# A decoder layer on one core: expert sums, sorted rows' transposes, mask waits and the last chunk's loads in another order

## What is computed

```python
    x = _layernorm(x + _L0_attn_ref(x, ...), axis=-1)                 # mixer: conv, GRU, feed-forward
    x = _layernorm(x + _L0_xattn_ref(x, ctx_1024, ctx_1024, ...), axis=-1)
    x = _layernorm(x + _L0_ffn_ref(x, ...), axis=-1)                  # shared expert + top 2 of 16
    # in the cross-attention
        scores = jnp.einsum('bthd,bshd->bhts', q, k)
        scores = scores + NEG_INF * (1.0 - causal)
        attn = jax.nn.softmax(scores, axis=-1)
        out = jnp.einsum('bhts,bshd->bthd', attn, v).reshape(B, T, H * Dv) @ Wo + bo
    # in the experts
        router_logits = jax.nn.sigmoid(x @ gate_w + gate_b)
        expert_values, expert_indices = jax.lax.top_k(router_logits, k=TOP_K)
        return x + _mlp(x, shared_wg, shared_wu, shared_wd) + expert_weighted
```

## Time and profile before

| | |
|---|---|
| time, median of 3 runs | 1507.69 us (1501.65 to 1508.32) |
| the profiled execution | 1508.78 us, its span 1507.0 us |
| PE busy | 1313.7 us (87%) |
| PE weight loads | 1079.7 us (72%) |
| DVE, ACT, POOL busy | 990.8 (66%), 939.4 (62%), 840.4 (56%) us |
| mean granted TensorE clock | 0.965 of full speed |
| PE's longest waits in total | 35.3 us for ACT's exponentials, 24.9 for POOL's xn, 21.1 for DVE's L1416 |

### The profile page before, as it was taken

The page is one execution under the profiler, slowest core; times in us unless marked ns, Lnnn a source line. Parts: engine busy times, 40 slices in busy tenths (PEclk is TensorE's granted clock), DMA queues, the critical chain, the costliest instruction groups (busy, mean ns, idle before and its releaser), DMA issues. The chain is left out here.

```text
span 1507.0 us, 34476 instructions
## 1 busy us (share of the span) xinstructions
PE 1313.7 (87%) x11280; PEld 1079.7 (72%) x11280; DVE 990.8 (66%) x2616; ACT 939.4 (62%) x3395; POOL 840.4 (56%) x988
## 2 busy tenths in 40 slices
PE   2889897989999999989999898989989899998752
PEld 1667686778787787767787787767778787777642
DVE  3456656565666767767776767677676777767535
ACT  2676766576675767577675667667666757756321
POOL 5343445653456555665476655676466645757454
PEclk9999999999999999999999999999999999999877
DMA  7000000033022222133121321223221331225673
GB/s 222 8 8 8 8 8 15 18 86 88 22 75 73 70 72 64 50 92 92 36 77 54 102 79 40 65 87 89 60 65 54 96 98 36 68 81 163 190 213 87
DMA packets 149426, 109.99 MB, mean 73 GB/s; under 512 B 12737, under 2 KB 144385, under 8 KB 149249
## 3 DMA queue, kind: packets, MB, share of 16 engines
q1 hardware_dynamic: 139328, 89.43, 20.4%
q0 software_dynamic: 8192, 16.79, 4.1%
q10 hardware_dynamic: 1728, 1.57, 0.4%
HBM read 73.14 MB, written 34.60 MB: 71 GB/s over the span
## 5 line engine op out<-in xcount | busy, mean ns | idle before, releaser
L1798 POOL TENSOR_TENSOR pr<-pr,ri 128x480 f32<-128x480 f32 x256 | 253.6, 1008 | 305.0 <-DVE ri L1399 303.1
L1073 ACT ACTIVATE pr<-sE,nm 128x120 f32<-128x120 f32 x512 | 178.0, 359 | 248.6 <-DVE nm L1394 247.7
L1073 ACT ACTIVATE pr<-sO,nm 128x120 f32<-128x120 f32 x512 | 179.3, 383 | 0.0
L672 PEld LDWEIGHTS sE<-kT,qT 64*128 64x128 f32 x1024 | 126.4, 191 | 53.8 <-issue 53.8
L705 PE MATMUL pvb<-pT,vv 120*64 120x128 f32 x2048 | 144.1, 284 | 22.2 <-DVE xa L1416 21.1
L1409 DVE TENSOR_TENSOR hT<-pvb,col 128x512 f32<-128x512 f32 x128 | 88.0, 687 | 109.0 <-PE pvb L705 108.4
L1061 ACT ACTIVATE pT<-t 120x512 f32<-120x512 f32 x256 | 143.3, 628 | 24.4 <-PE t L531 24.4
L672 PE MATMUL sO<-kT,qT 64*128 64x120 f32 x1024 | 150.4, 288 | 0.0
L672 PE MATMUL sE<-kT,qT 64*128 64x120 f32 x1024 | 150.4, 288 | 0.0
L705 PEld LDWEIGHTS pvb<-pT,vv 120*64 120x64 f32 x2048 | 116.6, 141 | 47.1 <-issue 42.7
L1827 POOL DMA_INDIRECT sorted_x<-x,slot x128 | 130.3, 1018 | 33.6 <-issue 33.2
(11 more groups left out here) (382 smaller groups left out, 3541.4 us busy)
## 6 DMA issues: line engine op xcount, KB each, us to landing
wq<-in_w_e SPq DMA_DIRECT2D x232, 128.0 KB
sorted_y<-yq SPq DMA_DIRECT2D x68, 256.0 KB, 2.6
xq<-sorted_x SPq DMA_DIRECT2D x58, 256.0 KB, 3.0
xt<-in_x SPq DMA_DIRECT2D x16, 256.0 KB, 3.0
sorted_x<-yq SPq DMA_DIRECT2D x16, 256.0 KB, 4.1
cT<-in_ctxT SPq DMA_DIRECT2D x16, 240.0 KB, 3.1
out_y<-y SPq DMA_DIRECT2D x48, 64.0 KB, 1.6
sorted_x<-x,slot POOLq DMA_INDIRECT x128
```

The lines of the kernel that those rows point to most:

```text
L672: ins = mm(score_banks[r][:, i * S:(i + 1) * S], qT[r * DK:(r + 1) * DK, j, q * T:(q + 1) * T], kT[r * DK:(r + 1) * DK, j, q * S:(q + 1) * ...
L1073: ins = f(pr[:, p % RING, r, i, :], score_banks[r][:, i * S:(i + 1) * S], ACT.Exp, bias=nm[:, p % 2, r, i:i + 1], accum_out=rsum[:, p % 2, ...
L1798: GP.tensor_tensor(pr[:, p % RING, r, :, :], pr[:, p % RING, r, :, :], ri[:, p % 2, r, :, :].to_broadcast([P, 4, S]), ALU.mult).then_inc(s ...
```

## The change

Six edits. (1) `b_scores`: each mask waits for its own bank's exponentials, not for both. (2) In slot 3 of bodies that have stages a and d, `d_T` of the next quad stands ahead of `b_scores`, no longer behind `b_pv`. (3) DVE: with one group in stage e, `e_sum` of the odd slots 3, 5, 7, 9 stands ahead of `b_heads_T` and the reciprocals, no longer behind `d_act`. (4) The two reciprocals of 128x4 are one of 128x8, which waits for both banks' exponentials; both `b_normal` wait for it. (5) SP in the tail: the six `x_load` of the last chunk stand ahead of `d_store(LAST + 3)` and the third `w_load`. (6) The last group's stores of sequences 1 and 3 are issued by ACT, those of 0 and 2 by SP.

```diff
@@ SP, tail
             w_load(n + 1)
+            for i in range(LONE_QUADS):
+                x_load(n + i)
             d_store(LAST + 3)
             w_load(n + 2)
-            for i in range(LONE_QUADS):
-                x_load(n + i)
...
-            for e in (TAIL + 2, TAIL + 3):
-                for q in range(SEQ):
-                    e_store(e, q)
+            for q in range(SEQ):
+                e_store(TAIL + 2, q)
+            for q in range(0, SEQ, 2):
+                e_store(TAIL + 3, q)
@@ PE, b_scores
-                if p:
-
-                    pe.wait_ge(sem["probs"], upto("probs", b, 2 * p - 1))
                 for r in range(2):
+                    if p:
+                        pe.wait_ge(sem["probs"], upto("probs", b, 2 * p - 2 + r))
                     mm(score_banks[r][:, 0:4 * S], identb[:], maskb[:].unsqueeze(1).to_broadcast([P, 4, S]),
@@ PE, body
                         b_probs_T(b, s - LAG)
+                    if up_in(d, s + 1) is not None and s == 3 and A:
+                        d_T(up_in(d, s + 1))
                     if B and 0 < s < PAIRS:
                         b_scores(b, s)
...
-                    if up_in(d, s + 1) is not None:
+                    if up_in(d, s + 1) is not None and not (s == 3 and A):
                         d_T(up_in(d, s + 1), c if s == 1 else None)
@@ ACT, end
+            for q in range(1, SEQ, 2):
+                act.wait_ge(sem["ln3_out"], upto("ln3_out", G - 1, q))
+                act.dma_start(out[(G - 1) * SEQ + q], y_of(G - 1, q)).then_inc(sem[f"out{q}_stored"], 16)
@@ DVE
-            def b_recips(b, p, r):
-                dve.wait_ge(sem["probs"], upto("probs", b, 2 * p + r))
-                V.reciprocal(ri[:, p % 2, r, :, :], rsum[:, p % 2, r, :, :]).then_inc(sem["rinv"], 1)
+            def b_recips(b, p):
+                dve.wait_ge(sem["probs"], upto("probs", b, 2 * p + 1))
+                V.reciprocal(ri[:, p % 2, :, :, :], rsum[:, p % 2, :, :, :]).then_inc(sem["rinv"], 1)
...
+                    if len(es) == 1:
+                        for e, q in sums_in(es, s):
+                            e_sum(e, q)
                     if B and s >= LAG:
                         b_heads_T(b, s - LAG)
                     if B and s < PAIRS:
-                        b_recips(b, s, 0)
-                    if B and s < PAIRS:
-                        b_recips(b, s, 1)
+                        b_recips(b, s)
...
-                    for e, q in sums_in(es, s):
-                        e_sum(e, q)
+                    if len(es) == 2:
+                        for e, q in sums_in(es, s):
+                            e_sum(e, q)
@@ POOL
             def b_normal(b, p, r):
-                pool.wait_ge(sem["rinv"], upto("rinv", b, 2 * p + r))
+                pool.wait_ge(sem["rinv"], upto("rinv", b, p))
```

More of the change, by code:

```diff
@@ L103 @@
     "ctx_hi": 1, "ctx_split": 1, "proj": 24, "proj_act": 12, "proj_dve": 12, "scores": 16, "negmax": 16, "probs": 16,
-    "probsT": 16, "probsT0_sb": 8, "probsT1_sb": 8, "rinv": 16, "normal": 16, "pv": 8, "headsT_sb": 8,
+    "probsT": 16, "probsT0_sb": 8, "probsT1_sb": 8, "rinv": 8, "normal": 16, "pv": 8, "headsT_sb": 8,
     "wo": 4, "attn_sum": 4, "ln2_stats": 4, "ln2_mv": 4, "ln2_eps": 4, "ln2_rstd": 4, "ln2_out": 4,
```

## The result

The changed kernel takes 1514.45 us (median of 7 runs, 1512.92 to 1516.96); the kernel before took 1507.69 us beside it. The ratio is 1.0051, 95% interval 1.0032 to 1.007: slower by half a percent, where 1497 us was forecast. The profiled execution lasted 1514.69 us.

The account below looks back on a forecast made before the run. PE's work plus its waits bound the kernel; +4.5 - 4.1 - 10 + 7.7 - 4.1 - 1.8 - 3.2 - 0.5 = -11.5 us against 1508.8 us gave 1497.3, predicted as 1497 us; own range 1492 to 1502, with rivals 1487 to 1511 us.

Parts of the forecast that it names:

- Slot 3, +4.5 us: Slot 3: bank masks and early transposes gain 0.6 us, but PE then waits for xn: +0.3 us in each of 15 bodies.
- The clock, -4.1 us: Slot 3, even bodies: clock falls cost 8.2 us; cutting PE's standstill in pieces takes half back, bounds 0 and -8.2 us.
- rival (a): Clock falls as before or at other places, so the 4.1 us stay: 1501.5 us, chance 0.17.
- Slots 5 and 6, -10 us: Slots 5 and 6: expert sum moves into DVE's idle time, so PE's waits for L1416 shrink by 10 us.
- a bound of -4 us: Slots 5 and 6: the smallest gain allowed there, if ACT's tanh is the next limit.
- Slots 7 and 8, +7.7 and -4.1 us: Earlier sum delays hT, PE waits 0.77 us in ten bodies; five waits of 0.82 us for xn in slot 8 go.
- The sorting chain, 0 us: Slot 1, even bodies: cast L1511 behind POOL's products, no change taken; bounds -0.8 and +1.0 us in seven bodies.
- rival (c): POOL's two products, released together, hold DVE at L1511 in slot 1 and the sum in slot 7: 1519 us, chance 0.14.
- L1511 over 1.1 us: Slot 1: the sign by which DVE would be seen waiting for both of POOL's products.
- Other masks, -1.8 us: Nine mask waits outside those of slot 3 in bodies 3 to 14 gain 0.2 us each.
- Tail, -3.2 and -0.5 us: Tail: rows loaded earlier let `d_up` start 3.2 us sooner; last four stores issued by two engines gain 0.5 us.
- rival (d): Tail: the loads only swap places, because the DMA engines are full: 1500 us, chance 0.08.

Follow-up runs that it names:

- a1_after: The changed kernel itself, run again on a chip as fast as the first: 1511.35 us, 1.0057 of the kernel before.
- c2: The kernel before with only the tail's two edits (rows' loads ahead of the third weights load, last stores on two engines), on a slower chip: 0.9997 of before.

## Why the prediction was wrong, point by point

Each term against the traces on the faster chip, before and after:

- **Slot 3, +4.5 us.** Right in kind, and in its working: the wait for xn was put at 0.9 us and reads 0.97 us. The slot costs 0.3 us in odd bodies (0.13 + 0.97 against 0.78) and 0.14 us in even ones, +2.6 us in bodies 5 to 14 and about nothing in bodies 0 to 4.
- **The clock, -4.1 us.** Wrong, and rival (a) right: 55 us at the half level ahead of the last scores, before and after. In this trace slot 3 of bodies 4 to 14 no longer falls, but slot 6 does, behind waits of 1.06 and 0.61 us. Windows of slots 3 and 6 in two even bodies (length, PE busy, granted clock, DMA share, GB/s):

```profile
751.00:761.00 10.00, 7.22 (x74) 1.00 0.17 48
925.00:935.00 10.00, 7.21 (x74) 1.00 0.17 49
...
777.00:787.00 10.00, 8.68 (x78) 0.83 0.10 28
951.00:961.00 10.00, 8.68 (x78) 0.83 0.10 28
```

  All four even bodies from 8 to 14 read so in this trace. In the second one of the same kernel (a1_after) slot 3 falls in bodies 4 and 14 in spite of mask and transposes, and slot 6 in bodies 8 and 10 only. Its body 14, slot 3, and bodies 8 and 12, slot 6:

```profile
1274.00:1284.00 10.00, 8.77 (x75) 0.83 0.19 48
777.00:787.00 10.00, 8.32 (x77) 0.83 0.14 42
1125.00:1135.00 10.00, 8.34 (x97) 1.00 0.17 50
```

  With two reciprocals PE waits 1.03 and 0.61 us at the same place in slot 6 and its clock stays. So neither the length of one wait nor what fills it decides alone; what does is not settled. The Trainium skill (TensorE: Matmul & The Clock Gate, Part 4: PE-mode transpose) says that transposes don't count as busy. Slot 3 with the transposes in its wait stayed at 1.00 in one trace and fell in two of six even bodies of the other, and the E mask, a matmul, was there too, so no run here shows it.
- **Slots 5 and 6, -10 us.** This step failed most: the waits for L1416 fell by 5.7 us in bodies 5 to 14 (1.07 us in each odd body, hardly anything in most even ones), and rose by 1.1 us in bodies 0 to 4. The text had a bound of -4 us, where ACT's tanh is next, and I took body 3 as the nearest row instead. In even bodies the next limit is POOL. In slot 5 of body 8, DVE's first operation on the tanh and POOL's operation beside it, before:

```profile
775.71 0.84 DVE L1320 TENSOR_SCALAR hin<-hin 128x512 f32<-128x512 f32 x1
775.07 1.20 POOL L1754 TENSOR_TENSOR cS_lo<-cT,cS_hi 128x480 fp32r<-128x480 f32 x1
```

  and in the changed kernel, with DVE up to L1421:

```profile
773.25 1.40 DVE L1325 TENSOR_SCALAR hin<-hin 128x512 f32<-128x512 f32 x1 [1.26 <-ACT hin L1015]
774.69 0.69 DVE L1327 SCALAR_TENSOR_TENSOR hin<-ma,hin 128x512 f32<-128x512 f32 x1
...
776.14 0.66 DVE L1399 TENSOR_REDUCE nm<-sE 128x4 f32<-128x480 f32 x1
776.71 0.65 DVE L1399 TENSOR_REDUCE nm<-sO 128x4 f32<-128x480 f32 x1
777.28 0.28 DVE L1421 TENSOR_TENSOR xa<-pvb,x1b 128x128 f32<-128x128 f32 x1
...
773.17 1.20 POOL L1761 TENSOR_TENSOR cS_lo<-cT,cS_hi 128x480 fp32r<-128x480 f32 x1
```

  DVE is now idle for 1.26 us for the tanh, a time which the sum used to fill. Behind the reciprocal L1325 does start 0.56 us earlier than before (1.46 us after it, not 2.02), but it takes 1.40 us instead of 0.84, and in both kernels it ends 0.28 us behind POOL's operation (774.65 and 774.37; 776.55 and 776.27). The same 0.28 to 0.29 us stand in bodies 6, 12 and 14 of both traces. The sum left the chain, and the chain ended no earlier: DVE's operation was held until POOL's was over.
- **Slots 7 and 8, +7.7 and -4.1 us.** Right in kind, the first too large: hT costs 0.50 us in nine of ten bodies rather than 0.77 us, 5.4 us in all, and the five waits of 0.82 us for xn went.

```profile
788.13 2.05 PE L714 MATMUL pvb<-wo,hT 128*128 128x128 f32 x16 [0.50 <-DVE hT L1414]
```

- **The same xn in slot 8 of bodies 0 to 2** is not in the sum. The one reciprocal delays the products there too: three waits of 0.9 us where 0.13 us stood, +2.4 us.

```profile
116.80 0.65 PE L532 MATMUL ma<-ident_f,xn 128*128 128x128 f32 x4 [0.89 <-POOL xn L1774]
```

  I had priced the reciprocal in slot 3 alone, though its text stands in all eight slots.
- **The sorting chain, 0 us.** Wrong, and inside the bound: L1511 (L1516 now) is free, 0.17 us, but the two behind it are held. +3.4 us over bodies 4 to 14: rival (c) in one of its two places, though its sign, L1511 over 1.1 us, pointed at the wrong operation. In its other place, slot 7, it did not act: the sum's operations read 0.34 and 0.35 us.
- **Other masks, -1.8 us.** Right: 3.3 us in bodies 0 to 2 became 1.8 us.
- **Tail, -3.2 and -0.5 us.** Nearly all missing, rival (d). PE's waits there (start, duration, idle before), answering to the earlier trace rows:

```profile
1460.10 1.12 PE L532 MATMUL t<-ident_f,kT 128*128 128x128 f32 x4 [3.63 <-DMA kT<-sorted_x]
...
1466.93 1.97 PE L823 MATMUL t<-xqT,qT 128*64 128x128 f32 x16 [4.86 <-DMA qT<-in_w_e]
```

  and SP:

```profile
1453.06 1.84 SPq L395 DMA_DIRECT2D kT<-sorted_x  x3
...
1457.93 0.82 SPq L420 DMA_DIRECT2D sorted_y<-yq  x1
1459.52 4.32 SPq L411 DMA_DIRECT2D qT<-in_w_e  x4
```

  The last scores come 6.3 us later than in the kernel before, and times of its tail compare less that. The rows are issued at 1446.8, as forecast. The third load of weights is issued at 1453.2 and not at 1451, 4.2 us later than before, since the six loads of rows and a store keep SP. 8.3 us of waiting became 3.6 + 4.9 us, and `d_up` starts at 1460.6 instead of 1462.3: of 3.2 us 1.7 us were there. They were lost behind it, where PE ran at the low clock for longer (the granted clock was 0.50 until 1465.3 before, and until 1472.5, in the time of the changed kernel, after). The same 16 matmuls, before and in the changed kernel:

```profile
1465.25 1.11 PE L823 MATMUL ma<-xn,qT 128*64 128x128 f32 x16
```

```profile
1469.88 1.98 PE L823 MATMUL ma<-xn,qT 128*64 128x128 f32 x16
```

  From the last scores (+6.3 us) to the end (+5.9 us) the tail gained 0.4 us. The DMA share reads 1.14 from 1460 to 1464 and 1.03 from 1464 to 1467 while PE waits for the weights, so the DMA engines are full there, as rival (d) had it. How much of the delay is theirs and how much the order on SP was not tested apart.

Put together: +5.4 us too little in slots 5 and 6, 4.1 of the clock, 3.4 of the chain, 2.4 of xn in slot 8, 3.3 of the tail, less 4.2 us that slots 3 and 8 cost less than forecast, is 14.4 of the 17.4 us between the forecast's -11.5 us and the +5.9 us of the profiled executions. Some 3 us stay without an owner. The same by edit: the forecast held the one reciprocal at some 11.5 us, since it turned -7 us of slot 3 into +4.5 us, and the rest of the change at -23 us. Measured, the reciprocal costs 20 us and the rest gains 14.3 us (1491.31 against 1505.62). So the forecast had both signs right and both sizes wrong (its two shares are an estimate of mine from its terms): the rest mostly by slots 5 and 6, the clock and the tail, and the reciprocal's cost by being priced in slot 3 alone, where slot 8 of bodies 0 to 2, the sorting chain and falls of the clock were added.

## What to carry to other kernels

An edit that merges two small operations into one delays the first half's readers and releases two long operations of the neighbouring engine together: look for every place where its text is executed, not for the one slot under study. When work is taken out of a chain, ask what holds the next operation: a sum that filled a wait for one engine, or a time in which a neighbour would have slowed the next operation, gains nothing by leaving. Compare two traces of the same kernel before a fall of the clock is put down to an edit. A change worth 1% can turn its sign with the chip, so a verdict on one holds for that chip.

## What was not expected of the hardware

On four of the chips the kernel before took 1573 to 1578 us, 4.5 to 4.8% more, though DVE's hT took 687 ns on the faster chip and 688 ns in c2. Two things are seen there. One is idle time with no releaser in the profile: in c2, DVE resumed at 784.45 and ACT at 784.51, though what they read had left PE at 781.99 (`b_pv`) and 782.58 (`d_T`) by the profile's modelled ends. PE's semaphores, for which they wait, are recorded at 784.43 and 784.49 in that trace, so DVE and ACT follow at once, and what is late is PE's signal, or PE itself behind its modelled ends (one slot earlier the signal of `b_pv` comes 0.02 us behind that end). The long ones come in the same slots of every second body. The other is the granted clock, 0.941 to 0.955 of full speed in all runs of before on these chips against 0.965 to 0.972 on the faster one, which at 2 x 0.02 x 1575 us is some 60 us more at the half level, worth up to 30 us (an estimate). What makes PE late, and whether the clock is lower for the same reason, is not settled by any run here.

In the first trace of the changed kernel PE's granted clock fell at the same two places of each pair of bodies from 8 on (slot 6 of the even, slot 1 or 2 of the odd one, 3.4 us at 1.2 GHz each), while a pair took 174.0 us; in its second trace some of these falls are missing, and with two reciprocals, where the pair takes 170.5 us, they come once per pair in bodies 7 to 13.
